# Nine mix products held to the end of the first aggregation, the one-tile group's gate work moved on, and a fetch marker for TensorE's branch

## The chip, the core and the metric

One core of one Trainium2 chip runs the kernel. The metric is device time in microseconds of one execution; the span in the profile runs from the first to the last instruction of the program. TensorE is called PE below, VectorE DVE, ScalarE ACT, GpSimd POOL and SyncE SP.

## What is computed

A graph of 3125 nodes (25 tiles of 128 rows, the last of 53) with 53125 weighted edges, 256 features a node. In short:

```python
xn = layernorm(x)
spmm = lambda z: segment_sum(edge_weight[:, None] * z[src], dst)     # A @ z
h = spmm(xn)                                                         # first aggregation
A0 = softmax(spmm(h) @ W0.T + b0); A1 = softmax(spmm([A0, A0]) @ W1.T + b1)
gnn = tanh(concat([A0, A1]) + h)                                     # 4 equal heads, mean
mix = linear attention of xn, folded to xn @ M + bo                  # M is 256 x 256
x = x + gnn + mix
probs = softmax(layernorm(x) @ gate_w + gate_b)                      # 8 experts
idx = argmax(probs); pos = place of the token in its expert's queue, kept if pos < 489
x = x + expert_ffn(idx, layernorm(x)) * probs[idx] * kept            # 256 -> 1024 -> 256
```

## The kernel before, in words

Five engine programs run side by side and meet at semaphores. Each engine takes its instructions in the order written.

**Build and first aggregation.** `UNITS` are 163 pieces of the dense adjacency matrix (strips of 512 columns of 4 tiles; strip 5 has 3 tiles, strip 6 the tiles 23 and 24). One loop over `it` runs on every engine. For each unit DVE makes one-hot operands (`hots`), PE multiplies them into a PSUM bank (`build`, L1555), ACT copies the block to the ring buffer and stores it to HBM (`evac`), and PE applies it to the normalised features (`apply`, L1571) into the banks `ACC` and `ACC + 1` (3 and 4). After a strip ACT and DVE copy these banks out (`strip_out`), and for each tile PE transposes and projects (`hidden_node`, L1463, L1587, L1588) and DVE copies the result (`hn_out`). Between these stand the mix products: `mix(m)` on PE (L1595) multiplies tile m of the transposed features by M, two f32 matmuls, which the profile shows as four instructions, and `mixed(m)` on DVE (L1113) adds the result to `X1`. `MIX_AT` places `mix(0)` to `mix(21)` at it = 40, 44, ..., 124. After the loop PE's order is mix(22), hidden_node(23), mix(23), hidden_node(24), mix(24).

**The branch.** A general path for unusual edge lists stands behind `more_rounds(pe)` (L458, L459): PE loads the register `rounds`, compares, and jumps over the whole body. With the inputs given the body isn't run. SP, POOL and DVE have the same branch over bodies of their own.

**Second and third aggregation.** `strip(l, k, inserts)` (L1720) runs 25 products per strip against adjacency chunks that SP reads back from HBM into a ring of five slots (L586); l = 0 has 7 strips, l = 1 has 8 (`Z1`). In strips 5, 6 and 7 of l = 1, named ka, kb and kc, the tiles are [20, 21], [22] and [23, 24]. Work for earlier strips is put between the products by `inserts`, keyed by the product's number j. `turns` (L1736) multiplies a finished strip by W1, DVE and ACT make the softmax (`biased` L1282, `ex` L852, `summed` L1291, `tanh` L858, `finished` L1298), `gate_turn` (L1463) transposes, ACT copies (`xtout`, L869), `logits` (L1756) multiplies by the gate weights, DVE picks the expert (`chosen`), `counts` (L1765 and on) makes running counts on PE, `slotted` (L1362 to L1366) makes the row numbers, and POOL scatters the rows (L686, L693). Tiles 22, 23 and 24 form one gate group. `zout` (L845) is ACT's copy of a finished strip. After that PE runs 11 filler products (`WARM`, L1823) and the eight experts (L1808, L1820), which need the scattered rows read back (`tokens`) and transposed (L1448).

Of the kernel before, what the change touches and what calls it, by code (L numbers as in the profile page):

```python
# [16 lines left out]
D = 256  # L17
H = 128
P = 128
NT = 25  # L20
# [103 lines left out]
for _t in range(NT - 2):  # L124
    _k, _i = _t // 4, _t % 4
    HN_AT[NT * _k + 30 + (5 * _i if _k < 5 else _i)] = _t
MIX_AT = {40 + 4 * _m: _m for _m in range(NT - 3)}
KV_AT, T1_AT, M_AT, FOUND_AT = 33, 37, 39, 60

def ge(eng, semaphore, value):

    if not isinstance(value, int) or value > 0:
        eng.wait_ge(semaphore, value)

def graph_program(nc, a, out):
    ctx = ExitStack()
    with ctx:
# [17 lines left out]
        XN, X1 = XX[:, :, 0:D], XX[:, :, D:2 * D]  # L157
        kp, ids = XX[:, :, 2 * D], XX[:, :, 2 * D + 1].bitcast(I32)
        XT = sb("XT", [P, 2, NP])
# [114 lines left out]
        rounds = sb("rounds", [1, 1], I32)  # L274
# [15 lines left out]
        M = W[:, 3364:3876].rearrange("p (c n) -> p c n", c=2)  # L290
# [25 lines left out]
        ps = ctx.enter_context(nc.psum_tensor("ps", [P, 8, 512], F32))  # L316
# [6 lines left out]
        HNB = 5  # L323
        MIXB = 6
        TURN = (2, 7)
        mix_bank = lambda m: MIXB if m < NT - 2 else ACC + m - (NT - 2)
        XTB = 3
        LGB = 5
        CNB = 6
# [125 lines left out]
        @contextmanager  # L455
        def more_rounds(eng):

            count = eng.value_load(rounds[0:1, 0:1], min_val=1, max_val=2)  # L458
            with eng.If(count > 1):  # L459
                with eng.Fori(1, count) as k:  # L460
                    yield k
# [252 lines left out]
        def _(act):  # L714
# [123 lines left out]
            def zout(l, k):  # L838
                w = width((STRIPS, Z1)[l][k])
                act.wait_ge(s_zc, Z_ENDS[l][k])  # L840
                ge(act, s_zt[l], k - 1)
                if l == 0:
                    nc.scalar.activation(zts[k % 2][:, 0:w], ps[:, k % 2, 0:w], ACT.Identity, bias=cols[:, 0:1]).then_inc(s_zev[l], 1)
                else:
                    nc.scalar.copy(zts[k % 2][:, 0:w], ps[:, k % 2, 0:w]).then_inc(s_zev[l], 1)  # L845
# [9 lines left out]
            def tanh(l, k):  # L855
                w = len((STRIPS, Z1)[l][k])
                act.wait_ge(s_sum[l], k + 1)
                nc.scalar.activation(tbuf[k % 2][:, 0:w, :], tbuf[k % 2][:, 0:w, :], ACT.Tanh).then_inc(s_tanh[l], 1)  # L858
# [13 lines left out]
            def exp8(k):  # L872
                t = slice(GATES[k][0], GATES[k][-1] + 1)
                act.wait_ge(s_tb, k + 1)
                nc.scalar.activation(ta8[:, t, :], tb8[:, t, :], ACT.Exp).then_inc(s_exp8, 1)
# [19 lines left out]
            zout(1, kb)  # L895
            ex(1, kb)
            tanh(1, kb)
            exp8(ka)
            xtout(kb)
            zout(1, kc)  # L900
            ex(1, kc)
            tanh(1, kc)
            xtout(kc)
# [21 lines left out]
        def _(dve):  # L925
# [182 lines left out]
                v.tensor_copy(Y[:, t, :], ps[:, HNB, D:D + H]).then_inc(s_hrd, 1)  # L1108

            def mixed(m):  # L1110
                dve.wait_ge(s_mixp, m + 1)
                dve.wait_ge(s_bo, m + 1)
                v.tensor_tensor(X1[:, m, :], X1[:, m, :], ps[:, mix_bank(m), 0:D], ALU.add).then_inc(s_mrd, 1)  # L1113

            heads = lambda x: x.rearrange("p (h d) -> p h d", d=HD)
            g_v = gvb[:, 0, :].unsqueeze(1).to_broadcast([P, 2, HD])
# [94 lines left out]
                if it - 3 in MIX_AT:  # L1211
                    mixed(MIX_AT[it - 3])
            strip_out(NS - 1)
            mixed(NT - 3)
            hn_out(NT - 2)
            mixed(NT - 2)
            hn_out(NT - 1)
            mixed(NT - 1)

            with more_rounds(dve):
# [238 lines left out]
        def _(pe):  # L1460
# [128 lines left out]

            def mix(m):  # L1590
                pe.wait_ge(s_mv, 1)
                if m < NT - 2:
                    ge(pe, s_mrd, m)
                for c in range(2):
                    last = nc.tensor.matmul(ps[:, mix_bank(m), 0:D], XT[:, c, m * P:(m + 1) * P], M[:, c, :], start=(c == 0), stop=(c == 1))  # L1595
                last.then_inc(s_mixp, 1)

            turn(0)
# [1 line left out]
            for it in range(NU + 4):  # L1600
# [40 lines left out]
                    hidden_node(HN_AT[it])  # L1641
                if it in MIX_AT:
                    mix(MIX_AT[it])
            mix(NT - 3)
            hidden_node(NT - 2)
            mix(NT - 2)
            hidden_node(NT - 1)
            mix(NT - 1)

            with more_rounds(pe):
                pe.wait_ge(s_hrd, NT)
                pe.wait_ge(s_mrd, NT)
                pe.sem_inc(m_mm, 1)
                pe.sem_inc(m_app, 1)

                def edges(start):
                    for q in range(8):
                        last = nc.tensor.matmul(ps[:, q, 0:CHUNK], e_dot, e_row[:, q * CHUNK:(q + 1) * CHUNK], start=start, stop=True, skip_group_check=True)
                    last.then_inc(m_mm, 1)  # L1660
                with pe.Fori(0, NT) as j:
                    pe.wait_ge(m_add, j + 1)
                    pe.wait_ge(m_pair, j * ET + 1)
                    edges(True)
                    with pe.Fori(1, ET) as c:
                        pe.wait_ge(m_pair, j * ET + c + 1)
                        edges(False)
                pe.wait_ge(m_add, NT + 1)

                def rows(w, tiles, loaded, across=512, first=0):  # L1670
                    pe.wait_ge(m_chunk, loaded)
                    for i, j in enumerate(tiles):
                        for dd in range(2):
                            last = nc.tensor.matmul(ps[:, ACC + dd, 0:w], XN[:, j, dd * H:(dd + 1) * H], e_chunk[:, i * across + first:i * across + first + w],
                                                    start=(j == 0), stop=True, skip_group_check=True)
                    last.then_inc(m_app, 1)

                def outs(k, w):
                    pe.wait_ge(m_hev, k + 2)
                    for i in range(w):  # L1680
                        pe.wait_ge(m_hrd, k * 4 + i + 1)
                        nodes(hTs[0], i)
                        last_of_nodes[0].then_inc(m_hnt, 1)
                with pe.Fori(0, NS - 1) as k:
                    pe.wait_ge(m_hev, k + 1)
                    for c in range(5):
                        rows(512, range(c * 5, c * 5 + 5), (k * 5 + c + 1) * 16)
                    outs(k, 4)
                pe.wait_ge(m_hev, NS)
                rows(LAST, range(0, ENDN), 31 * 16, ENDW, P)  # L1690
                rows(LAST, range(ENDN, NT), 32 * 16, ENDW, P)
                outs(NS - 1, 1)
                pe.wait_ge(m_hrd, NT + 1)

            def strip(l, k, inserts):
# [30 lines left out]
            def turns(l, k):  # L1727
                b = k % 2
                pe.wait_ge(s_zev[l], k + 1)
                if k >= 2:  # L1730
                    pe.wait_ge(s_ex[0] if l == 0 else s_nm[1], k - 1)
                elif l == 1:
                    pe.wait_ge(s_ex[0], NS - 1 + k % 2)
                for i in range(len((STRIPS, Z1)[l][k])):
                    o, z = ps[:, TURN[b], i * P:(i + 1) * P], zts[b][:, i * P:(i + 1) * P]
                    last = flip(o, z) if l == 0 else nc.tensor.matmul(o, z, W1T[:, :], start=True, stop=True)  # L1736
                last.then_inc(s_zt[l], 1)

            def gate_turn(k):
                pe.wait_ge(s_x1, k + 1)  # L1740
                ge(pe, s_xtb, k)
                for j in Z1[k][DOT_TILES if k < DOTS else 0:]:
                    i = j - GATES[gate_of(k)][0]
                    for c in range(2):
                        last = flip(ps[:, XTB + i // 2, i % 2 * D + c * P:i % 2 * D + (c + 1) * P], X1[:, j, c * P:(c + 1) * P])
                last.then_inc(s_gturn, 1)

            def logits(k):
                g = gate_of(k)
                pe.wait_ge(s_xtb, k + 1)  # L1750
                pe.wait_ge(s_gwc, 2)
                ge(pe, s_lgr, g)
                for j in Z1[k][DOT_TILES if k < DOTS else 0:]:
                    i = j - GATES[g][0]
                    for c in range(2):
                        last = nc.tensor.matmul(ps[:, LGB, i * NE:(i + 1) * NE], xtb[g % 2][:, i, c * P:(c + 1) * P], gate_w[:, c, :], start=(c == 0), stop=(c == 1))  # L1756
                last.then_inc(s_lg, 1)
# [17 lines left out]
            def later(f, *args):  # L1775
                return lambda: f(*args)
# [12 lines left out]
                    inserts[23] = [later(gate_turn, k - 1)]  # L1789
                strip(1, k, inserts)  # L1790
            strip(1, ka, {1: [later(logits, ka - 2)], 3: [later(turns, 1, ka - 1)], 15: [later(counts, ka - 2)], 21: [later(gate_turn, ka - 1)]})
            strip(1, kb, {3: [later(turns, 1, ka)], 4: [later(logits, ka - 1)], 14: [later(counts, ka - 1)], 22: [later(gate_turn, ka)]})
            strip(1, kc, {4: [later(turns, 1, kb)], 5: [later(logits, ka)], 21: [later(counts, ka), later(gate_turn, kb)]})
            turns(1, kc)
            logits(kb)
            gate_turn(kc)
            logits(kc)
# [52 lines left out]
```

## Time and profile before

| | |
|---|---|
| runs of before | 1148.77, 1150.28 and 1151.73 us, median 1150.28 |
| profiled execution | 1142.74 us, span 1141.0 us, mean granted clock 0.978 |
| PE / DVE / ACT / POOL busy | 94% / 65% / 28% / 14% of the span |
| first aggregation ends on PE | at 594.9 us |
| first product of the second aggregation | at 600.5 us |
| last product of the third aggregation | at 890.6 us |
| first expert product | at 913.3 us |

All places are microseconds from the start of the span. A granted clock of 1.00 is 2.4 GHz and 0.50 is 1.2 GHz. A merged timeline row gives start, duration from the first to the last of its instructions, what it is, and in brackets the idle time ahead of it and what ended that.

### The profile page before, as it was taken

To read this page: it belongs to the slowest core of one execution; us is meant where nothing else is said; L and a number is where in the kernel's file an instruction comes from. 1 tells how busy PE (TensorE), PEld (TensorE's weight loads), DVE (VectorE), ACT (ScalarE), POOL (GpSimd) and SP (SyncE) were. 2 spreads that over 40 slices of the span, in tenths; PEclk is the share of its full clock that TensorE was granted. 3 is DMA by queue.
4 is the path that set the end of the run, shared out by engine and by line. 5 is a ranking of instruction groups with operands and counts; after the bars stand their busy time and mean duration, and the time that the engine had idled before them with its cause. 6 is when DMAs were issued, how large, how long until landed. Compare 5 with 4: busy or idle time off the path is not lost.

```text
span 1141.0 us, 15390 instructions
## 1 busy us (share of the span) xinstructions
PE 1071.9 (94%) x5383; PEld 666.5 (58%) x5383; DVE 738.9 (65%) x1860; ACT 314.7 (28%) x1042; POOL 163.2 (14%) x208
## 2 busy tenths in 40 slices
PE   5869989999999999999979999999998799999995
PEld 3446656656666666666774444644458566666664
DVE  8978999998786887869950111217877445544444
ACT  4657867522222222222210111201112112222220
POOL 1113223301000000000000000000344511111111
PEclk9889999999999999999998999999999899999998
DMA  6111110111324333342348988987994665555510
GB/s 173 16 12 47 47 47 18 76 82 76 146 115 153 122 133 136 131 167 105 139 160 314 361 309 301 358 319 281 311 327 171 179 194 125 136 137 133 147 51 8
DMA packets 78877, 178.60 MB, mean 157 GB/s; under 512 B 33567, under 2 KB 62011, under 8 KB 66639
## 3 DMA queue, kind: packets, MB, share of 16 engines
q1 hardware_dynamic: 67550, 126.16, 34.4%
q10 hardware_dynamic: 7120, 43.34, 9.4%
q0 software_dynamic: 4128, 8.08, 2.0%
q8 instruction: 45, 0.74, 0.3%
q14 instruction: 34, 0.27, 0.1%
HBM read 116.23 MB, written 63.77 MB: 158 GB/s over the span
## 4 chain that ended last, share of the span: by engine, by line
PE 77%; DVE 11%; SPq 4%; issue 4%; ACT 2%; DMA 1%; POOLq 0%; POOL 0%; ACTq 0%; DVEq 0%
PE ps L1720 21%; PE ps L1571 20%; PE ps L1820 10%; PE ps L1808 9%; PE ps L1555 7%; SPq L477 2%; PE ps L1595 2%; PE ps L1530 2%; PE ps L1463 1%; PE ps L1516 1%; PE ps L1550 1%; DVE RING L1096 1%; DVE RING L1087 1%; DVE W L1039 1%; SPq L475 1%
## 5 line engine op out<-in xcount | busy, mean ns | idle before, releaser
L1571 PE MATMUL ps<-RING,XX 128*128 128x512 f32 (+2 forms) x700 | 297.1, 550 | 2.0 <-DVE W L1103 2.0
L1720 PE MATMUL ps<-RING,RY 128*128 128x512 f32 (+4 forms) x750 | 272.1, 520 | 5.7 <-issue 5.7
L1720 PEld LDWEIGHTS ps<-RING,RY 128*128 128x128 f32 x750 | 135.7, 194 | 125.7 <-issue 118.3
L790 ACT COPY RING<-ps 128x512 f32<-128x512 f32 (+3 forms) x163 | 91.0, 559 | 291.6 <-PE ps L1555 266.3
L1571 PEld LDWEIGHTS ps<-RING,XX 128*128 128x128 f32 x700 | 118.1, 191 | 69.9 <-issue 62.1
L1096 DVE TENSOR_TENSOR RING<-RING,RY 128x768 bf16<-128x768 bf16 x275 | 142.7, 560 | 4.0
L1555 PEld LDWEIGHTS ps<-RING 128*128 128x128 bf16 x1575 | 100.6, 97 | 50.0 <-issue 43.3
L1087 DVE TENSOR_TENSOR RING<-iota_p,RY 128x512 bf16<-128x512 bf16 x275 | 114.1, 456 | 18.1 <-PE ps L1555 15.7
L1555 PE MATMUL ps<-RING 128*128 128x128 bf16 (+1 forms) x1575 | 112.9, 217 | 0.0
L916 ACT ACTIVATE RY<-ps,b1T 128x489 f32<-128x489 f32 x64 | 42.8, 669 | 172.4 <-PE ps L1808 172.4
L1436 DVE SCALAR_TENSOR_TENSOR W<-ps,RING,W 128x256 f32<-128x256 f32 (+1 forms) x32 | 15.5, 484 | 99.0 <-PE ps L1820 97.8
L1267 DVE TENSOR_REDUCE nmx<-ps 128x4 f32<-128x512 f32 (+2 forms) x7 | 4.4, 635 | 111.7 <-PE ps L1463 111.7
L686 POOL DMA_INDIRECT xbuf_dram<-XX,sidx x25 | 25.1, 1004 | 326.8 <-DVE sidx L1366 321.0
L709 POOL DMA_INDIRECT out<-W,RING x32 | 31.4, 981 | 189.3 <-DVE W L1443 165.0
L672 POOL TENSOR_TENSOR XX<-XX,bo_b 128x256 f32<-128x256 f32 x25 | 21.3, 851 | 244.3 <-PE ps L1555 244.2
L1820 PE MATMUL ps<-XT,RY 128*128 128x256 f32 (+1 forms) x256 | 55.9, 379 | 0.0
L1820 PE MATMUL ps<-RING,RY 128*128 128x256 f32 (+1 forms) x256 | 55.9, 379 | 0.0
L1530 PE MATMUL ps<-wkvT,XT 128*128 128x512 f32 x100 | 50.3, 628 | 4.9 <-ACT XT L752 4.9
L1808 PE MATMUL ps<-RING,XT 128*128 128x489 f32 x128 | 53.2, 574 | 0.5 <-DVE RING L1448 0.5
L1808 PE MATMUL ps<-RING 128*128 128x489 f32 x128 | 53.1, 573 | 0.0
L1820 PEld LDWEIGHTS ps<-RING,RY 128*128 128x128 f32 (+1 forms) x256 | 47.5, 186 | 9.2 <-issue 1.8
L1820 PEld LDWEIGHTS ps<-XT,RY 128*128 128x128 f32 (+1 forms) x256 | 47.5, 185 | 9.2 <-issue 1.8
(265 smaller groups left out, 1313.5 us busy)
## 6 DMA issues: line engine op xcount, KB each, us to landing
RING<-adj_dram SPq DMA_DIRECT2D x60, 1280.0 KB, 6.4
adj_dram<-RING ACTq DMA_DIRECT2D x30, 1280.0 KB, 4.8
rbuf_dram<-W SPq DMA_DIRECT2D x8, 516.0 KB, 5.1
RING<-rbuf_dram SPq DMA_DIRECT2D x8, 516.0 KB, 4.0
xbuf_dram<-W SPq DMA_DIRECT2D x8, 512.0 KB, 3.2
XT<-in_L_ffn_w SPq DMA_DIRECT2D x16, 256.0 KB, 5.2
XT<-in_L_ffn_w SPq DMA_DIRECT2D x4, 1024.0 KB, 8.6
RING<-in_L_ffn_w SPq DMA_DIRECT2D x16, 256.0 KB, 4.5
```

The costliest lines, as they stand in the source:

```text
L686: gp.indirect_dma_start(xbuf_dram[:, :], bass.IndirectOffsetOnAxis(ap=sidx[:, j:j + 1], axis=0), XX[:, j, 0:D], None, bounds_check=NE * XS ...
L709: gp.indirect_dma_start(out[:, :], bass.IndirectOffsetOnAxis(ap=rbs[0:n, e % 2, c, D + 1:RES].bitcast(I32), axis=0), ybs[0:n, e % 2, c, :] ...
L790: nc.scalar.copy(RING[:, n % 2, at:at + w], ps[:, u % 2, 0:w]).then_inc(s_bev, 1)
L916: nc.scalar.activation(hmT[:, f, 0:CAPX], ps[:, 2 + f % 3, 0:CAPX], ACT.Relu, bias=b1T[:, f, e:e + 1]).then_inc(s_hidv, 1)
L1087: last = v.tensor_tensor(h[:, 0:4:3], every.unsqueeze(1).to_broadcast([P, 2, P, fields.shape[-1]]), wide(fields[:, 0:2], 2), ALU.is_equal)
L1096: last = v.tensor_tensor(h[:, 1:4], h[:, 3:4].to_broadcast([P, 3, P, fields.shape[-1]]), wide(fields[:, 2:5], 3), ALU.mult)
L1530: last = nc.tensor.matmul(ps[:, PROD, :], XT[:, c, m * P:(m + 1) * P], wkvT[:, c, :], start=(c == 0), stop=(c == 1))
L1555: last = nc.tensor.matmul(o[:, c:c + w], piece(0, i, P), piece(1 + f, i, w), start=(f == 0), stop=(f == 2 and j != s))
L1571: last = nc.tensor.matmul(ps[:, ACC + dd, 0:w], XN[:, j, dd * H:(dd + 1) * H], at[:, i * w:(i + 1) * w], start=(j == 0), stop=True, skip_g ...
L1720: last = nc.tensor.matmul(o, (Y if l == 0 else S0)[:, j, :], RING[:, slot_of[g % 5], i * across + first:i * across + first + w], start=(j ...
L1808: last = nc.tensor.matmul(ps[:, 2 + f % 3, 0:CAPX], w1s[s][:, c, f * P:(f + 1) * P], xbT[:, s, c, 0:CAPX], start=(c == 0), stop=(c == 1))
L1820: last = nc.tensor.matmul(o, hmT[:, f, c * P:c * P + n], w2s[s][:, f, :], start=(f == 0), stop=(f == 7))
```

## The change

Three edits.

1. `HELD = 16`: only `mix(0)` to `mix(15)` stay in the loop. `mix(16)` to `mix(24)` run after it. They no longer share one bank: `HELD_AT` gives them halves of the banks MIXB, KVACC, PROD, ACC and ACC + 1, so that none waits for DVE to clear another. DVE adds all nine after its last `hn_out`, waiting for both halves of a bank. Since KVACC and PROD are the banks in which `turns` of the second aggregation writes, `turns(0, 0)` and `turns(0, 1)` get a wait for all 25 additions.
2. `more_rounds(pe)` is written out as a wait, the register load, and a compare-and-branch that carries a hint. The hint's place in the instruction stream (`over_general`) is ahead of `hidden_node(24)`.
3. In strips kb and kc PE's inserts are moved: `counts(ka - 1)` and `gate_turn(ka)` from strip kb to strip kc, `turns(1, kb)` and `logits(ka)` later in strip kc, `counts(ka)` and `gate_turn(kb)` behind `turns(1, kc)`. ACT's `zout(1, kc)` goes ahead of `exp8(ka)` and `xtout(kb)`.

```diff
-MIX_AT = {40 + 4 * _m: _m for _m in range(NT - 3)}
+HELD = 16
+MIX_AT = {40 + 4 * _m: _m for _m in range(HELD)}
...
-        mix_bank = lambda m: MIXB if m < NT - 2 else ACC + m - (NT - 2)
+        HELD_AT = ((MIXB, 0), (MIXB, D), (KVACC, 0), (KVACC, D), (PROD, 0), (PROD, D), (ACC, 0), (ACC, D), (ACC + 1, 0))
+
+        def mix_out(m):
+            bank, at = HELD_AT[max(m - HELD, 0)]
+            return ps[:, bank, at:at + D]
+
+        def mixes_to_bank(m):
+            return m + 1 if m < HELD else max(n for n in range(HELD, NT) if HELD_AT[n - HELD][0] == HELD_AT[m - HELD][0]) + 1
... ACT
+            zout(1, kc)
             exp8(ka)
             xtout(kb)
-            zout(1, kc)
... DVE
-                dve.wait_ge(s_mixp, m + 1)
+                dve.wait_ge(s_mixp, mixes_to_bank(m))
...
             strip_out(NS - 1)
-            mixed(NT - 3)
             hn_out(NT - 2)
-            mixed(NT - 2)
             hn_out(NT - 1)
-            mixed(NT - 1)
+            for m in range(HELD, NT):
+                mixed(m)
... PE
-                if m < NT - 2:
-                    ge(pe, s_mrd, m)
+                ge(pe, s_mrd, min(m, HELD))
...
-            mix(NT - 3)
+            mix(HELD)
             hidden_node(NT - 2)
-            mix(NT - 2)
+            mix(HELD + 1)
+            over_general = pe.mark_branch_hint_location()
             hidden_node(NT - 1)
-            mix(NT - 1)
-
-            with more_rounds(pe):
+            for m in range(HELD + 2, NT):
+                mix(m)
+
+            pe.wait_ge(s_rounds, 1)
+            count = pe.value_load(rounds[0:1, 0:1], min_val=1, max_val=2)
+            pe.br_lt(count, 2, "pe_edges_done", "pe_edges_general").branch_hint(over_general)
+            with nc.body("pe_edges_general", ...), pe.Fori(1, count):
...
+            nc.switch_bb("pe_edges_done")
... turns
+                if l == 0 and k < 2:
+                    pe.wait_ge(s_mrd, NT)
...
-            strip(1, kb, {3: [later(turns, 1, ka)], 4: [later(logits, ka - 1)], 14: [later(counts, ka - 1)], 22: [later(gate_turn, ka)]})
-            strip(1, kc, {4: [later(turns, 1, kb)], 5: [later(logits, ka)], 21: [later(counts, ka), later(gate_turn, kb)]})
+            strip(1, kb, {3: [later(turns, 1, ka)], 4: [later(logits, ka - 1)]})
+            strip(1, kc, {4: [later(counts, ka - 1)], 6: [later(gate_turn, ka)], 13: [later(turns, 1, kb), later(logits, ka)]})
             turns(1, kc)
+            counts(ka)
+            gate_turn(kb)
             logits(kb)
             gate_turn(kc)
             logits(kc)
```

## Rows read from the trace of the kernel before

**Rows 1.** The page, part 1: busy time of each engine.
```profile
PE 1071.9 (94%) x5383; PEld 666.5 (58%) x5383; DVE 738.9 (65%) x1860; ACT 314.7 (28%) x1042; POOL 163.2 (14%) x208
```

**Rows 2.** Stretches: length, PE, PEld, DVE, ACT, POOL busy (instructions), clock, DMA share, GB/s.
```profile
450.00:500.00 50.00, 50.00 (x338) 31.30 (x338) 41.59 (x102) 10.54 (x18) 4.35 (x5) 1.00 0.45 165
515.00:540.00 25.00, 25.00 (x177) 17.37 (x177) 24.52 (x58) 5.74 (x12) 1.74 (x2) 1.00 0.26 107
...
595.00:600.50 5.50, 0.00 (x0) 0.00 (x0) 0.34 (x1) 0.00 (x0) 0.00 (x0) 0.80 0.94 388
600.50:605.10 4.60, 4.57 (x6) 2.02 (x7) 0.00 (x0) 0.00 (x0) 0.00 (x0) 0.50 0.69 235
605.10:609.70 4.60, 4.60 (x12) 2.00 (x11) 0.00 (x0) 0.00 (x0) 0.00 (x0) 1.00 0.98 398
...
895.20:900.80 5.60, 3.05 (x14) 2.56 (x15) 4.63 (x26) 2.34 (x6) 0.00 (x0) 0.50 1.07 327
```

**Rows 3.** The chain in the loop and at its end: start, us, what.
```profile
457.93 0.86 PE ps L1595 x4
...
590.82 0.86 PE ps L1595 x4
...
594.88 5.66 issue
```

**Rows 4.** Lines L458 and L459: duration in ns, first start in us.
```profile
L459 SPq COMPARE_BRANCH  x1: 50/50/50, 482.0 to 482.0; - x1
...
L459 PEldq COMPARE_BRANCH  x1: 6295/6295/6295, 594.1 to 594.1; - x1
L459 DVEq COMPARE_BRANCH  x1: 76/76/76, 596.0 to 596.0; - x1
```

**Rows 5.** Instruction packets in the stretch 597.5 to 600.5 us: packets, MB, share.
```profile
q8 instruction: 1, 0.02, 2.0%
```

**Rows 6.** DVE's timeline at the end of the third aggregation (and one addition).
```profile
594.91 0.42 DVE L1113 TENSOR_TENSOR XX<-XX,ps 128x256 f32<-128x256 f32 x1 [0.24 <-PE ps L1595]
...
883.21 0.29 DVE L1282 TENSOR_TENSOR W<-ps,gb_b 128x128 f32<-128x128 f32 x1 [0.78 <-PE ps L1736]
...
889.50 0.17 DVE L1362 TENSOR_TENSOR wkvT<-ps,last_e 128x16 f32<-128x16 f32 x1 [1.98 <-PE ps L1773]
...
891.74 0.42 DVE L1282 TENSOR_TENSOR W<-ps,gb_b 128x256 f32<-128x256 f32 x1 [1.45 <-PE ps L1736]
```

**Rows 7.** PE's timeline over the strips kb and kc and behind them.
```profile
870.47 2.48 PE L1720 MATMUL ps<-RING,RY 128*128 128x128 f32 x20
876.76 0.19 PE L1765 MATMUL ps<-wkvT,upto_b 128*128 128x32 bf16 x1 [3.81 <-DVEq L1343]
...
879.23 1.06 PE L1463 MATMUL ps<-ident,XX 128*128 128x128 f32 x4
...
883.32 0.95 PE L1756 MATMUL ps<-gate_w,XT 128*128 128x8 f32 x8
884.13 5.18 PE L1720 MATMUL ps<-RING,RY 128*128 128x181 f32 x32
...
890.99 0.71 PE L1736 MATMUL ps<-W1T,W 128*128 128x128 f32 x4 [0.40 <-ACT W L845]
...
897.20 1.88 PE L1756 MATMUL ps<-gate_w,XT 128*128 128x8 f32 x8 [0.74 <-ACT XT L869]
...
900.89 11.95 PE L1823 MATMUL ps<-RY,ident 128*128 128x512 f32 x22
913.31 1.06 PE L1808 MATMUL ps<-RING,XT 128*128 128x489 f32 x2 [0.47 <-DVE RING L1448]
```

**Rows 8.** POOL's timeline: the first scatter of the last gate group.
```profile
902.76 0.97 POOL L686 DMA_INDIRECT xbuf_dram<-XX,sidx  x1 [7.99 <-DVE sidx L1366]
```

**Rows 9.** SP's timeline: the loads of strip kc's two chunks.
```profile
868.96 3.23 SPq L586 DMA_DIRECT2D RING<-adj_dram  x2
```

**Rows 10.** Line L586, all chunk loads: time from issue to landing.
```profile
DMA to landing us min/median/max: 5.3/6.3/13.0
```

More of the change, by code:

```diff
@@ L1110, in mixed @@
             def mixed(m):
-                dve.wait_ge(s_mixp, m + 1)
+                dve.wait_ge(s_mixp, mixes_to_bank(m))
                 dve.wait_ge(s_bo, m + 1)
-                v.tensor_tensor(X1[:, m, :], X1[:, m, :], ps[:, mix_bank(m), 0:D], ALU.add).then_inc(s_mrd, 1)
+                v.tensor_tensor(X1[:, m, :], X1[:, m, :], mix_out(m), ALU.add).then_inc(s_mrd, 1)
             heads = lambda x: x.rearrange("p (h d) -> p h d", d=HD)
@@ L1591, in mix @@
                 pe.wait_ge(s_mv, 1)
-                if m < NT - 2:
-                    ge(pe, s_mrd, m)
+                ge(pe, s_mrd, min(m, HELD))
                 for c in range(2):
-                    last = nc.tensor.matmul(ps[:, mix_bank(m), 0:D], XT[:, c, m * P:(m + 1) * P], M[:, c, :], start=(c == 0), stop=(c == 1))
+                    last = nc.tensor.matmul(mix_out(m), XT[:, c, m * P:(m + 1) * P], M[:, c, :], start=(c == 0), stop=(c == 1))
                 last.then_inc(s_mixp, 1)
@@ L1643, in _ @@
                     mix(MIX_AT[it])
-            mix(NT - 3)
+            mix(HELD)
             hidden_node(NT - 2)
-            mix(NT - 2)
+            mix(HELD + 1)
+            over_general = pe.mark_branch_hint_location()
             hidden_node(NT - 1)
-            mix(NT - 1)
-            with more_rounds(pe):
+            for m in range(HELD + 2, NT):
[3 more added lines that the diff above has]
+            pe.br_lt(count, 2, "pe_edges_done", "pe_edges_general").branch_hint(over_general)
+            with nc.body("pe_edges_general", valid_engines=bass.OrderedEngineSet([pe.engine])), pe.Fori(1, count):
                 pe.wait_ge(s_hrd, NT)
```

## The prediction

> **What bounds the kernel now.** I read the page's busy shares first: PE works 94% of the span and no other engine over 65% [rows 1], so what counts is where PE stands still or runs at a low clock, and which engine it then waits for. Next come the stretches. From 450 to 500 us, where the last mix products of the loop stand, PE is busy 50.00 of 50 us while DVE has 8 us free; from 515 to 540 us PE is still full, but DVE is nearly so too [rows 2]. The reader is to see that the loop is paced by PE in both. Then the chain: a mix product is worth 0.86 us of PE in the loop and 0.86 us behind it, and behind the last one stands the longest idle piece of the PE-bound part, 5.66 us put down to "issue", which is no semaphore [rows 3]. The rows of the branch's line name it: the compare-and-branch takes 0.05 us on SP, 0.08 on DVE and 6.30 us on PE, from 594.1 us on [rows 4]. In that time one packet of instructions comes in, late, while the DMA engines are 94% busy at 388 GB/s with chunk loads and stores [rows 2, 5]. Behind the hole the granted clock is 0.50 (1.2 GHz) until 605.1 us, and PE does six instructions in 4.6 us where it then does twelve [rows 2]. Last come the timelines of the end of the third aggregation. From 870 us on PE is no longer the bound: it waits 3.81 us for DVE's one-hot rows with strips kb and kc still to do, and then DVE waits for PE three times, 0.78, 1.98 and 1.45 us, before its last softmax starts at 891.74 us [rows 6, 7]. The chain from there to the first expert product at 913.31 us goes through DVE, ACT, PE, POOL's scatter and the read-back, and each link waits for the one before.
>
> **Edit 1, the held products.** Six products (16 to 21) leave the loop: 6 x 0.86 = 5.16 us of PE come off a stretch in which PE never waits [rows 2, 3]. The same six come back behind the loop, again 5.16 us, with PE full on both sides. Sum 0. DVE loses six additions of 0.42 us [rows 6] from the loop, where they were hidden; one of them, for product 21, falls into the stretch where DVE is nearly full, so at most 0.42 us is gained there; I take 0. At the end DVE makes nine additions, 9 x 0.42 = 3.8 us and about 0.5 us for the last one after PE's last product. Queued behind them on DVE is only its branch and the first reduction of the second aggregation, which needs `turns(0, 0)`. The new wait for all 25 additions stands in `turns(0, 0)`, behind 25 + 8 products of strip 0 and 1: at twelve instructions in 4.6 us [rows 2] and two instructions a product that is 66 x 0.38 = 25 us after the first product. It costs nothing; if the cover were gone it would cost the half microsecond. The products write six different half banks and wait for no addition after the sixteenth, so PE runs them at 0.86 us each. SP's queue: its chunk loads are released by the last build and the last apply, both 5.16 us earlier, and PE's first strip starts about as long after them as now, so that the loads have the same lead.
>
> The Trainium skill (Runtime: NRT & Kernel Launch, Instruction fetch mechanics) says that a taken branch whose target is not in the fetch window forces a DMA fetch before execution can go on. The trace agrees: 6.30 us and a packet of instructions. The same section says "Prefetch is purely sequential"; by that rule the marker could not bring the target early, and edit 2 would be worth 0; no row here has a marked branch.
>
> **Edit 3, the gate work.** In the trace's own time, from 870.47 us on. PE does the last 20 products of strip kb in one go: twice the 2.48 us of ten of them gives 875.4 us, where now the wait of 3.81 us stands between. Strip kc's 25 products are 50 instructions at 5.18/32 = 0.162 us, 8.1 us. Between them go counts(ka - 1), whose one-hots come at 876.76 us, when PE is at kc's fifth product (877.0), so it doesn't wait; gate_turn(ka), at most 1.06 us; turns(1, kb), 0.4; logits(ka), 0.95 [rows 7]. Strip kc ends at about 886.1 us instead of 890.6. These durations hold the tails of pipelined groups; by the instructions' distance it is 884.7.
>
> DVE decides the rest. Its order is unchanged. It is free for kb's softmax 0.78 us before it gets turns(1, kb), and turns(1, kb) is now done by about 881 us, so 0.78 us is saved. slotted(ka) then waits for counts(ka), which PE now has behind turns(1, kc): ACT's copy at 885.0 to 886.4, turns(1, kc) 0.7 us [rows 7], counts at 885.9 to 887.5. DVE asks for it at 889.50 - 1.98 - 0.78 = 886.74 us [rows 6]. So of the 1.98 us between 1.2 and all is saved. turns(1, kc) is then long done, and the 1.45 us are saved too. The sum is 3.4 to 4.2 us [rows 6]; I take 4.0, nearer the end that the instructions' distance gives. ACT's moved copy is what lets turns(1, kc) run before xtout(kb); xtout(kb) and exp8(ka) have until the last logits. POOL's queue: the scatter of the last group starts 7.99 us after POOL's last work [rows 8] and may come 4 us earlier without a collision. SP's queue: the loads of kc's two chunks are released by kb's fifth and tenth product, which do not move. The first is needed at 875.4 us; a load takes 5.3 to 13.0 us, median 6.3, from 868.96 us on [rows 9, 10], so the median lands in time and the slowest would be 6.6 us late. The filler products take 11.95 us and end 0.5 us before the experts can start [rows 7]; they move with the chain. But behind 895.2 us the clock is at 0.50 [rows 2], and if it rises later against the chain than now, the fillers end up to 1 us late; if it is at 1.00 the last logits, 1.88 us for eight against 0.95 for eight [rows 7], win 0.9 us. I take 0 and keep 1 us either way for the range.
>
> **The sum.** 0 + 5.66 + 2.3 + 4.0 = 12.0 us. The profiled execution would go from 1142.74 to 1130.7 us. The runs of before have a median 7.5 us above that execution; I take the difference as the same and get 1150.28 - 12.0 = 1138.3 us.
>
> **The rivals.**
> - The marker does nothing: PE stands 5.7 us at the branch and the clock falls as now. For it: nothing in the trace shows a fetch asked for ahead. Against it: between marker and branch there are 6.9 us and the fetch needs 6.3. Time: 1150.28 - 4.0 = 1146.3 us. A fetch that lands late by some microseconds gives a time between this and the forecast, and is counted here. Chance 0.13. The Trainium skill's rule of sequential prefetch, named above, would lead to this case.
> - The gate work gives nothing, because PE waits for kc's first chunk (a landing near the maximum of [rows 10]), or the counts come late. Time: 1150.28 - 7.9 = 1142.4 us. Against it: landings are mostly near the median. Chance 0.09.
> - Slower: the marked fetch takes the place of the block that PE needs next in sequence. PE then runs dry among the held products, for 6.30 us [rows 4] with the clock falling behind it (2.3 us), and the branch still costs its 5.7 and 2.3 us. It decides only if both fetches are paid: 1150.28 - 4.0 + 8.6 = 1154.9 us. Against it: PE's ordinary block fetches leave no hole in 50 us of loop [rows 2]. Chance 0.05.
> - Both gains fail and nothing is lost: about 1150 us, chance 0.05.
>
> **How the numbers follow.** The forecast has 0.68; its own range is 1136 to 1141 us (gate work 3.4 to 4.2, 0.4 us in the loop, 1 us of clock either way, 1 us of measurement). With the two cases of one gain the range is 1135.5 to 1146.5 us, which leaves out 0.15. A change under 0.3% (3.5 us) can't be told from none in this kernel. Faster by more: 0.68 + 0.13 + 0.09 = 0.90, less a case of a weak single gain, 0.89. Within 0.3%: 0.06. Slower: 0.05.
>
> **What the profile after would show.** The branch's row on PE at some 0.1 us in place of 6.3, no idle piece behind the last mix product, and a clock of 1.00 through the first strip. The last apply about 5.2 us earlier and nine mix products in a row with hidden nodes between, 0.86 us each. No wait for L1765 in strip kb; DVE's idle time ahead of L1282 and L1362 gone, and 21.6 us from the start of the last softmax (L1282) to the first expert product, as now. It is wrong if the branch's row stays at microseconds, if a hole opens elsewhere in the held products, if L1720 waits for a chunk in strip kc, or if the filler products end after the transposes.

## The result, and the profile after

The changed kernel takes 1138.07 us (median of 4 runs, 1137.69 to 1140.0) beside 1150.36 us of before: 12.3 us less between the medians. The ratio of the means is 0.9897 (interval 0.988 to 0.9914), which is 11.8 us. The forecast was 1138.3 us and 12.0 us less. All ratios below leave out three executions of early_marker that took 1864 to 4980 us, and the profile of the first of them, at a granted clock of 0.56, is not used.

The profile of this run, though, is only 4.6 us shorter than the profile shown of before: the span is 1136.4 us against 1141.0. So it has to be read by stages. Four places cut the span: the first mix product (first L1595, now L1601), the first product of the second aggregation and the first of the third (L1720, now L1732), and the first expert product (L1808, now L1824).

| stage, us | before | after | difference |
|---|---|---|---|
| start to first mix product | 266.22 | 265.02 | -1.2 |
| to the second aggregation | 334.31 | 328.61 | -5.7 |
| second aggregation | 136.92 | 134.66 | -2.3 |
| third aggregation and gate, to the first expert | 175.86 | 180.42 | +4.6 |
| experts to the end | 227.69 | 227.69 | 0.0 |

The first stage holds no changed work, so its 1.2 us are not the change's. The next two are the hole (PE's idle time at its branch) and the clock behind it, to the tenth of a microsecond. The fourth is longer where 4 us less were forecast. First the part that went as said. These are the stretches of the loop and behind it, with columns as in [rows 2]:

```profile
450.00:500.00 50.00, 50.00 (x337) 29.77 (x336) 42.91 (x105) 11.15 (x19) 5.07 (x5) 1.00 0.47 175
515.00:540.00 25.00, 25.00 (x178) 17.05 (x177) 24.56 (x60) 6.11 (x13) 0.92 (x1) 1.00 0.38 158
585.00:593.60 8.60, 8.60 (x46) 7.19 (x45) 4.23 (x12) 0.00 (x0) 0.00 (x0) 1.00 1.00 384
593.60:598.60 5.00, 5.00 (x13) 2.37 (x13) 0.45 (x2) 0.00 (x0) 0.00 (x0) 1.00 0.59 199
```

PE is full in the loop as before [rows 2], full through the held products, and the second aggregation starts at a clock of 1.00. PE's timeline shows the seam, and the rows of the two lines show marker and branch (duration in ns, first start in us):

```profile
587.49 6.21 PE L1601 MATMUL ps<-W,XT 128*128 128x256 f32 x28
593.63 2.81 PE L1732 MATMUL ps<-RING,RY 128*128 128x512 f32 x6
```

```profile
L1653 PEldq BRANCH_PREFETCH_HINT  x1: 55/55/55, 585.1 to 585.1; - x1
...
L1661 PEldq COMPARE_BRANCH  x1: 2918/2918/2918, 590.5 to 590.5; - x1
```

Seven products in 6.21 us, and no idle time ahead of L1732, where [rows 3] had 5.66 us. But the branch takes 2.92 us and not 0.1. It starts at 590.5 us, when PE still has 3.2 us of products in its queue, and so hides: the sequencer, which takes in PE's instructions and runs the branch (its rows are those of PEldq), is that far ahead of the array. Now the part that did not go as said, DVE's timeline and PE's over the strips kb and kc:

```profile
868.29 0.42 DVE L1305 TENSOR_TENSOR XX<-XX,W 128x256 f32<-128x256 f32 x1
...
874.05 0.19 DVE L1369 TENSOR_TENSOR wkvT<-ps,last_e 128x32 f32<-128x32 f32 x1 [1.83 <-remote]
...
886.40 0.17 DVE L1369 TENSOR_TENSOR wkvT<-ps,last_e 128x16 f32<-128x16 f32 x1 [6.35 <-remote]
```

```profile
862.07 6.25 PE L1732 MATMUL ps<-RING,RY 128*128 128x128 f32 x50
...
868.43 0.18 PE L1787 MATMUL ps<-wkvT,ones_b 128*128 128x32 bf16 x1
...
872.39 0.47 PE L1732 MATMUL ps<-RING,RY 128*128 128x181 f32 x2 [0.96 <-issue]
...
883.74 0.17 PE L1787 MATMUL ps<-wkvT,ones_b 128*128 128x16 bf16 x1
```

The 3.81 us wait for the counts is gone, PE runs 50 instructions in 6.25 us. But L1369 waits for L1787, the last product of `counts`, and starts at 874.05 us where that product is on record at 868.43, and at 886.40 where it is at 883.74. The profile calls the releaser "remote": it finds no event that fits. These late signals are in neither the prediction nor the profile of before. The question for the experiments was whether the 12 us are those that were argued, and what the late signals do to them.

### The profile page after: what moved, and what is told of

It is laid out like the page before. It is cut to its first block, busy times and chain, and to the rows that moved or that the text cites. A ratio compares the mean times of both kernels' runs of the same rounds, so it can differ in the third digit from the quotient of the medians.

```text
span 1136.4 us, 15395 instructions
## 1 busy us (share of the span) xinstructions
PE 1071.8 (94%) x5383; PEld 666.0 (59%) x5383; DVE 739.0 (65%) x1860; ACT 315.2 (28%) x1042; POOL 160.9 (14%) x208
## 4 chain that ended last, share of the span: by engine, by line
PE 77%; DVE 12%; SPq 4%; issue 3%; ACT 2%; another core or an unknown queue 1%; DMA 1%; POOLq 0%; DVEq 0%
PE ps L1578 20%; PE ps L1732 20%; PE ps L1836 10%; PE ps L1824 9%; PE ps L1562 7%; PE ps L1601 2%; SPq L485 2%; PE ps L1537 2%; PE ps L1523 1%; PE ps L1470 1%; PE ps L1557 1%; DVE RING L1104 1%; PE ps L1839 1%; DVE RING L1095 1%; DVE W L1047 1%
## 5 line engine op out<-in xcount | busy, mean ns | idle before, releaser
L1732 PE MATMUL ps<-RING,RY 128*128 128x512 f32 (+4 forms) x750 | 271.1, 518 | 1.8 <-issue 1.6
L1732 PEld LDWEIGHTS ps<-RING,RY 128*128 128x128 f32 x750 | 135.3, 193 | 121.2 <-issue 113.7
L1824 PE MATMUL ps<-RING,XT 128*128 128x489 f32 x128 | 53.2, 574 | 0.4 <-issue 0.4
L1824 PE MATMUL ps<-RING 128*128 128x489 f32 x128 | 53.1, 573 | 0.0
```

Source lines behind the costliest of these rows:

```text
L1732: last = nc.tensor.matmul(o, (Y if l == 0 else S0)[:, j, :], RING[:, slot_of[g % 5], i * across + first:i * across + first + w], start=(j ...
L1824: last = nc.tensor.matmul(ps[:, 2 + f % 3, 0:CAPX], w1s[s][:, c, f * P:(f + 1) * P], xbT[:, s, c, 0:CAPX], start=(c == 0), stop=(c == 1))
```

## The experiments

Ratios are to before on the same chip, in the same hours. Before took 1151.13 us on one chip and 1143.25, 1142.55 and 1143.46 us on three others. All stages below are from one profile each.

### Before again

> The kernel before, unchanged, for a second profile and for the noise. The profiled execution of before took 1142.74 us and its timed runs 1148.8 to 1151.7 us; the profile of the changed kernel took 1138.14, a typical time of it. Theory A (both parts of the change gain in each execution): a new profile of before of 1149 to 1151 us has its extra 7 to 8 us ahead of strip kb of the third aggregation, spread over the stages. Theory B (late signals): in the profile of the changed kernel PE's semaphore increments came 3 to 6 us late in two places behind strip kb, which cost about 8 us; a typical execution of before has such places too, and its extra 7 to 8 us lie between strip kb and the first expert product, whose distance is 46 us in the fast profile. Ratio of the times 1.000 in both.

Ratio 0.9986 (0.9974 to 0.9998), profile of 1148.2 us. The stages are 266.08, 334.42, 136.89, 183.17 and 227.69 us: all of the extra 7 us lie in the fourth. The waits of DVE from 860 to 905 us, first here, then in the first profile of before (total us, times, longest):

```profile
DVE W L1282 <- remote: 7.7, 2, 7.2
...
DVE wkvT L1331 <- remote: 2.6, 1, 2.6
DVE W L1282 <- PE ps L1736: 0.8, 1, 0.8
```

```profile
DVE wkvT L1362 <- PE ps L1773: 2.5, 2, 2.0
DVE W L1282 <- PE ps L1736: 2.2, 2, 1.5
```

So the late signals belong to before as much as to after. Five profiles have them: this one, that of the changed kernel and those of the next three experiments. The first profile of before and the eight later ones have none. The two levels of before, 1151 and 1143 us, fit this: the profile with late signals is of an execution of 1150.65 us, the one without of 1142.74 us. That it holds for the three chips at 1143 us is argued from other kernels' profiles there, since before wasn't profiled on them. The baseline for the changed kernel's first profile is this one, not the one shown ahead: against it the stages differ by -1.1, -5.8, -2.2, -2.8 and 0 us, together 11.9. Of these 10.8 us lie in stages with changed work.

### Held products and marker, gate work as it was

```diff
 (the changed kernel)
-            zout(1, kc)
             exp8(ka)
             xtout(kb)
+            zout(1, kc)
... and the inserts of strips kb and kc as before
```

> Held products and marker (edits 1 and 2), with the gate work where it was. Theory A: 7.9 us faster than before (5.66 of the hole behind the branch, 2.3 of the clock), about 1142.4 us, branch row under 3 us and no idle piece ahead of the first product of the second aggregation. Theory B agrees on this part; it differs on what edit 3 then adds. Rival C (layout: the whole gain comes from where PE's work falls against the late signals): not 7.9 but anything from 0 to 12 us.

Ratio 0.9927 (0.9913 to 0.994), 8.4 us. The stages are 266.97, 328.79, 134.66, 183.81 and 227.60 us: -5.6 and -2.2 us in the second and third against before again, 7.9 us with the hole gone and the clock kept. The branch's row is 3.04 us where under 3 was expected, and of the hole 0.15 us is left (595.61 to 595.76):

```profile
591.78 3.83 PE L1601 MATMUL ps<-W,XT 128*128 128x256 f32 x17
595.76 4.53 PE L1732 MATMUL ps<-RING,RY 128*128 128x512 f32 x10
```

### The gate work alone

```diff
 (the kernel before)
-            strip(1, kb, {3: [later(turns, 1, ka)], 4: [later(logits, ka - 1)], 14: [later(counts, ka - 1)], 22: [later(gate_turn, ka)]})
...
+            strip(1, kb, {3: [later(turns, 1, ka)], 4: [later(logits, ka - 1)]})
...
```

> The gate work moved (edit 3) alone. Theory A: 3.4 to 4.2 us faster than before, about 1146.3 us; the distance from the last instruction of strip kb's first five products to the first expert product falls from some 43 to some 39 us. Theory B: the gain in an execution depends on whether PE's signals come late behind strip kb: where they do in both kernels, 4 us are still gained; where they come late only in the changed order, because PE no longer rests in strip kb, up to 4 us are lost against the fast profile of before.

Ratio 0.9969 (0.9958 to 0.9981), 3.6 us; the fourth stage is 178.66 us against 183.17, so 4.5 us less. The two parts add up: 8.4 + 3.6 = 12.0, measured together 11.8. This profile has late signals too (DVE waits for L1362 2.0 and 3.6 us), so the 4.5 us are a difference between two stages with late signals; after_again, below, gives the size without them.

### The marker alone, 1.7 us of work ahead of the branch

```diff
 (the kernel before)
             mix(NT - 2)
+            over_general = pe.mark_branch_hint_location()
             hidden_node(NT - 1)
             mix(NT - 1)
... the branch as in the changed kernel
```

> The marker alone, put ahead of hidden_node(24), with only that and mix(24) between it and the branch, 1.7 us of PE work. Theory A (the marker starts the fetch): the branch's row falls from 6.3 us by 1.7 to 2.5 us, to some 4 us, the hole from 5.66 to some 3.5 us; the clock may still fall; 2 to 4 us faster. Rival (the marker does nothing, and the sequencer was only further ahead in the changed kernel): the row stays at 6.3 us and the time at that of before.

Ratio 0.9991 (0.9982 to 1.0001): nothing that can be told. The branch's row:

```profile
L1654 PEldq COMPARE_BRANCH  x1: 5558/5558/5558, 592.0 to 592.0; - x1
```

The marker stands at 589.16 us, so the target was there 8.4 us behind the marker, where an unmarked branch has it after 6.3 (6.40 in before again). The marker's 2.9 us ahead bought 0.8 us of branch; the hole is 5.06 us. The expectation of 1.7 to 2.5 us was wrong: the fetch is not of a fixed length. Most of the 0.7 us of hole is lost again behind it: the granted clock is 0.50 from 596.5 to 603.4 us, and as PE's products start at 597.75 us, more of them fall under it than in before. The second aggregation takes 137.46 us, 0.6 more than in before again.

### The held products alone

```diff
 (the changed kernel, gate work as before)
-            over_general = pe.mark_branch_hint_location()
...
-            pe.br_lt(count, 2, "pe_edges_done", "pe_edges_general").branch_hint(over_general)
...
+            with more_rounds(pe):
```

> The nine held products (edit 1) alone, with the branch as before. Theory A: no change, since PE is full where the six products leave and where they come back: ratio 1.000 within the 0.15% by which before repeats itself; the branch's row stays near 6.3 us, the hole near 5.7 us or, as PE's sequencer now runs up to 3 us ahead of the products without a wait, some 3 us. In the second case 2 to 3 us of the gain put down to the marker belong to the held products. Rival: held products cost their 5.2 us, ratio 1.0045.

Ratio 0.995 (0.9935 to 0.9964), 5.7 us faster: the expected ratio of 1.000 failed, and the second case of the hole came. PE's timeline and the branch's row:

```profile
588.90 6.21 PE L1601 MATMUL ps<-W,XT 128*128 128x256 f32 x28
597.91 6.66 PE L1727 MATMUL ps<-RING,RY 128*128 128x512 f32 x11 [2.80 <-issue]
```

```profile
L467 PEldq COMPARE_BRANCH  x1: 5742/5742/5742, 591.9 to 591.9; - x1
```

PE's products end at 595.11 us against 594.88 in before, so they themselves cost nothing. But seven products without a wait let the sequencer run ahead. It reaches the branch 3.2 us before PE runs dry, where [rows 3, 4] had 0.8, and the hole is 2.80 us. The low clock behind it is shorter too: the granted clock is back at 1.00 by 602.2 us, and the second aggregation takes 136.36 us, 0.6 less. Hole and clock make 2.9 + 0.6 = 3.5 us. The timed 5.7 us (4.1 to 7.4) are more than that; what the rest is, this profile doesn't show.

### The marker alone, early

```diff
 (the kernel before, branch as in the changed kernel)
             for it in range(NU + 4):
+                if it == NU:
+                    over_general = pe.mark_branch_hint_location()
                 if it < NT:
```

> The kernel before with the marked branch alone, the marker four iterations ahead of the loop's end, some 9 to 10 us of PE work ahead of the branch; no product is held. Theory A (all that counts is that the fetch starts more than 6.3 us ahead): the branch's row under 3 us, no or little hole (PE's sequencer is only 0.8 us ahead there, so up to 2 us may be left), 5 to 8 us faster, about 1143 us. Rival (the held products are what closes the hole): no more than the marker alone gave, 1150 us.

Ratio 0.9926 (0.9907 to 0.9945). The rows are those of the same kernel's second profile:

> Before with the marker alone, four iterations ahead of the loop's end, for a profile at full clock (the first one of this kernel was taken in a disturbed execution at a clock of 0.56). Branch row 0.1 to 0.5 us, since in four profiles the target was there 7.7 to 9.7 us behind the marker and here some 9.7 us of work stand between; hole under 0.5 us, clock 1.00 through the first strip, ratio 0.993.

Ratio 0.9926 (0.9908 to 0.9944), 8.5 us. PE's timeline and the branch:

```profile
593.91 1.03 PE L1595 MATMUL ps<-W,XT 128*128 128x256 f32 x4
594.96 5.39 PE L1726 MATMUL ps<-RING,RY 128*128 128x512 f32 x12
```

```profile
L1655 PEldq COMPARE_BRANCH  x1: 493/493/493, 594.3 to 594.3; - x1
```

No hole, the second and third stage are 328.66 and 134.67 us, and no product was moved. The whole gain of edits 1 and 2 is to be had from the marker. What the held products did in the change was to put the marker 5.5 us ahead of the branch on the sequencer where marker_only has 2.9, and to lengthen PE's queue at the branch from 0.8 to 3.2 us.

### The scatters left out, and some moved

The first of these two kernels leaves the scatters of gate groups 0 to 5 out, so that the experts get mostly blank rows; the second moves four of them.

```diff
 (the changed kernel, POOL; in the first, waits for s_disp and s_dres count the last group alone)
-            for k in range(NGT - 2):
-                scatter(k)
-                scatter_rest(k)
...
+            scatter(NGT - 1)
+            scatter_rest(NGT - 1)
```

> The changed kernel without the scatters of the first six gate groups; only the last group's rows are scattered, the waits count those alone, so the experts work on mostly blank rows. Theory D (PE's signals come late behind strip kb while GpSimd's scatters are under way, and only then): no PE signal over 1 us late, the stretch from strip kb to the first expert product falls from 49.9 to some 43 us, 5 to 8 us faster than the changed kernel, about 1131 us. Rival E (they come late from PE's own dense short instructions or from the chunk loads): late signals stay, 1137 to 1138 us.

```diff
 (the changed kernel, POOL)
-            for k in range(NGT - 2):
+            for k in range(NGT - 3):
                 scatter(k)
                 scatter_rest(k)
... and NGT - 3 in the two loops behind it
```

> The changed kernel with the second scatters (the residual rows) of gate group 4 moved behind the last group's first scatters. Theory D: four scatters fewer while strips kb and kc run, so fewer late signals, 1 to 4 us faster than the changed kernel, about 1135 us; the residual rows of expert 0 come 5 us later, still ahead of their use some 14 us after the first expert product. Rival E: the same as the changed kernel, or slower by the wait of DVE for the residual rows.

Ratios 0.9861 (0.9843 to 0.9879) and 0.9886 (0.9866 to 0.9906), on a chip where held_only has no late signal either. Both fail as tests of the cause: there was nothing to take away. Against the changed kernel run again (below) the first is shorter by 3.5 us in its span, and the experts to the end alone, with 224.09 us against 227.62, make these 3.5; of the other stages the first is 0.6 us shorter and the fourth 0.7 longer. That the blank rows cause it is likely, and wasn't looked into. Its fourth stage is 172.06 us, not shorter than 171.33. So where no signal is late, the scatters beside the strips cost nothing that the stages show. In the second kernel's profile the branch takes 2.14 us and leaves no hole, with the marker where the change has it.

### The changed kernel again

> The changed kernel, unchanged, beside the two below. So far before took 1151 us on one chip, whose profiles have late PE signals behind strip kb, and 1143 us on another, whose profiles have none. Theory A: on either, 12 us faster than before, ratio 0.9890; where no signal is late, the stretch from strip kb to the first expert product is 41.5 to 42.5 us against 46.1 in the first profile of before, where it is disturbed some 50 against 52.5. Theory B (the late signals give the gain): ratio 0.993 on a chip without them.

Ratio 0.9901 (0.9885 to 0.9917), 1132.06 against 1142.55 us. The stages are 266.77, 329.99, 134.66, 171.33 and 227.62 us. This is the profile to hold against the one of before: no signal is late in either. PE's timeline, then DVE's:

```profile
589.22 6.21 PE L1601 MATMUL ps<-W,XT 128*128 128x256 f32 x28
596.76 3.67 PE L1732 MATMUL ps<-RING,RY 128*128 128x512 f32 x8 [1.33 <-issue]
...
864.45 6.25 PE L1732 MATMUL ps<-RING,RY 128*128 128x128 f32 x50
870.74 0.19 PE L1779 MATMUL ps<-wkvT,upto_b 128*128 128x32 bf16 x1
...
879.74 0.17 PE L1779 MATMUL ps<-wkvT,upto_b 128*128 128x16 bf16 x1
...
890.49 12.43 PE L1839 MATMUL ps<-RY,ident 128*128 128x512 f32 x22
902.75 1.80 PE L1824 MATMUL ps<-RING,XT 128*128 128x489 f32 x4
```

```profile
876.30 0.29 DVE L1289 TENSOR_TENSOR W<-ps,gb_b 128x128 f32<-128x128 f32 x1
...
880.64 0.17 DVE L1369 TENSOR_TENSOR wkvT<-ps,last_e 128x16 f32<-128x16 f32 x1
...
881.35 0.41 DVE L1289 TENSOR_TENSOR W<-ps,gb_b 128x256 f32<-128x256 f32 x1
```

The three rows of DVE are those of [rows 6], and none has a bracket any more: the 0.78, 1.98 and 1.45 us are all gone. In the seam the branch takes 4.34 us here, and 1.33 us of hole are left, at a clock of 1.00.

> Four second scatters moved behind the last first scatters, as in rest_later, now beside the changed kernel. If the scatters make PE's signals late: 1 to 4 us faster than after_again on a chip with late signals, equal on one without. If they have no part in it: equal on both, ratio within 0.15% of after_again's.

Ratio 0.9896 (0.9879 to 0.9913), fourth stage 171.54 us against 171.33: the same as after_again, on a chip without late signals. What makes them is not told apart.

### The changed kernel with its marker early

```diff
 (the changed kernel)
-            over_general = pe.mark_branch_hint_location()
...
             for it in range(NU + 4):
+                if it == NU:
+                    over_general = pe.mark_branch_hint_location()
```

> The changed kernel with its marker at the fourth iteration from the loop's end, some 14 us of PE work ahead of the branch, instead of ahead of hidden_node(24). The target was there 7.7 to 9.8 us behind the marker in six profiles, against 6.3 us behind an unmarked branch; with the marker where the change has it, 0 to 1.35 us of hole were left. So: branch row under 0.5 us, hole under 0.1 us, up to 1.3 us faster than the changed kernel, ratio to before 0.989 on a chip without late signals (after_again had 0.9901 there). Rival (the block fetched early is gone again by the time of the branch, since PE takes in a further block of its own on the way): the row back at 6 us and a hole of 2.8 us as with held products alone, ratio 0.992.

Ratio 0.988 (0.9861 to 0.9898), 1129.67 us beside 1143.46. The branch's row is 0.40 us, and the hole is gone:

```profile
586.84 6.21 PE L1601 MATMUL ps<-W,XT 128*128 128x256 f32 x28
592.88 7.46 PE L1733 MATMUL ps<-RING,RY 128*128 128x512 f32 x17
```

Its second stage is 328.49 us against 329.99 of after_again, 1.5 us less. Part of it is lost again: the second aggregation takes 135.21 us against 134.66, and PE waits in it for a chunk that SP reads back, once, at 641 us, which no other profile has:

```profile
PE ps L1733 <- DMA RING<-adj_dram: 0.4, 1, 0.4
```

The intervals of the two ratios overlap, so the gain of the hole is shown by the rows, and that the whole is faster is not shown by the times. The rival, a target that is gone again by the time of the branch, didn't come. But it was hardly tested: from 580.5 to 593 us the trace has no instruction packet, so PE took in no other block between the target's and the branch.

## Why the prediction was right, point by point

**Edit 1, the sum of 0.** Right for the products (nine of them in nine half banks, where I wrote six): in held_only they end 0.23 us later than in before, with a first stage 0.23 us later too. Wrong for the edit as a whole, which alone gave 5.7 us. The step that failed is "PE's sequencer reaches the branch 0.8 us before the last product's end": I took this lead from before's order and kept it for the changed one, where it is 3.2 us. The 25 additions' wait cost nothing: the second aggregation has no idle time on PE ahead of its `turns` and takes 134.66 us.

**Edit 2, the hole.** "If the fetch is started at the marker it has landed when PE gets there, and the branch costs what it costs DVE, 0.08 us" was wrong twice. The marker-to-branch distance is 5.4 to 5.6 us on the sequencer in six profiles, not 6.9. The products from marker to branch do take 6.9 us of PE (in after_again from 588.53 to 595.43), but the sequencer is 1.7 us ahead of them at the marker and 3.2 us at the branch. And the target came 7.7 to 9.8 us behind the marker, not 6.3. So 2.1 to 4.3 us of branch were left. The hidden lead of 3.2 us swallowed all of it in the first profile and all but 1.33 us in the second. The sum's 5.66 us came out at 5.7 and 4.3 because two errors stood against each other; with the lead of 0.8 us that I had written, 1.3 to 3.5 us would have been left. So far the hit is luck. The credit is wrong too: the held products take 2.9 us of the hole without any marker.

**The clock.** Right: 2.3 us of [rows 2], measured 2.26 us (136.92 to 134.66) in both profiles of the changed kernel. Of the six other profiles with a hole of 1.35 us or less five have 134.58 to 134.67 us, and after_marker_early 135.21. The lower bound, a clock that falls anyway, did not come.

**Edit 3.** Right in its mechanism, and 0.5 us under-sized (after_again against the first profile of before). The last softmax starts 20.17 us behind strip kb's first product (861.18) against 24.53 us in before (867.21), 4.4 us where 3.4 to 4.2 were given; the first expert product comes 4.5 us earlier. kb and kc took what the instructions' distance said, not the durations: kb's last 20 products and kc ended at 878.8 us, 17.6 us behind kb's start against 23.4. All of the 1.98 us went, not 1.2. The filler products now end the stage: in before they ended 0.5 us ahead of the first expert product, here L1824 follows them at once. The prediction named this as a sign of being wrong. It cost little: the first expert product starts 0.99 us behind the first transpose (901.76 to 902.75 us), where in before it was 0.86 us (912.45 to 913.31).

**The sum and the baseline.** I made the sum against a profile of 1141.0 us and took the 7.5 us to the median as the same in both kernels. For the profile that failed: it was to take 1130.7 us and took 1138.14, 0.07 us from its median. Between medians the difference did hold: the ratio is 0.9897 where signals are late and 0.9901 where they are not. I had no reason for it from the trace, and the shape of the gain differs: 5.8 or 4.3 us of hole, 2.2 or 2.3 us of clock, 2.8 or 4.5 us of gate work. These make 10.8 or 11.1 us, not 12.0.

**The rivals.** No rival's time came about. But half of the first did: it counted "a fetch that lands late by some microseconds", and that is what happened in all six profiles with the change's marker, hidden, wholly in three of them and for the most part in the others, by a lead that neither the forecast nor the rival had. The marker does work: early_marker_2 has 0.49 us against 6.30. This is also the answer to the Trainium skill's sentence that prefetch is purely sequential (Runtime: NRT & Kernel Launch, Instruction fetch mechanics): a marked target comes in ahead of the branch, so the sentence does not hold for a branch with a hint. Its other sentence, that a far target forces a fetch, holds in all four profiles with an unmarked branch on PE (5.74 to 6.40 us). No chunk came late for strip kc, and no second fetch made a hole among the held products; between marker and branch the instruction queue moved only one packet, so this rival wasn't put to a test.

## What to carry to other kernels

- A far branch on a busy engine has three terms: when its fetch starts, how long the fetch takes in the DMA traffic of that moment, and how much work is queued in the engine when the sequencer gets there. Read the last from the branch's start against the end of the last product, in the order that will stand there, not in the one that does. Put the marker ahead of the large transfers, since behind them its packet came up to 4 us later: the plainest version, one marker and nothing moved, gave all 8 us.
- When the profiled execution stands several microseconds off the median, find the stage that holds the difference before a sum is made against it. A second profile of the same kernel costs little.
- Work that an in-order queue holds behind a wait is worth moving even when that queue isn't the bound: the idle brackets on the engine that is bound give the price, here 4.2 us read and 4.4 measured.

## What the runs showed of the hardware

**The fetch of a far target depends on what was handed to the DMA engines before it.** With the marker at 583.0 us (early_marker_2) the engines were 5% busy until 586.3 us, when the second of two instruction packets moved; with the marker at 586.8 us (after_again) they were 100% busy, and a single packet moved only behind 594 us. The stretches, columns as in [rows 2]:

```profile
583.00:586.30 3.30, 3.30 (x40) 3.25 (x37) 1.58 (x6) 0.92 (x2) 0.00 (x0) 1.00 0.05 10
```

```profile
586.80:594.20 7.40, 7.40 (x42) 6.38 (x41) 3.50 (x10) 0.00 (x0) 0.00 (x0) 1.00 1.00 377
```

And the instruction queue of after_again from 594 to 597 us, where there is none from 586 to 594:

```profile
q8 instruction: 1, 0.02, 2.0%
```

But busy engines alone don't make the wait: an unmarked branch finds them as busy and waits less. What goes with the wait is how long before the request the last of three large transfers was issued (two chunk loads of 1280 KB each and a store of 995 KB):

| asked for by | engines busy meanwhile | last large issue before it | packet moves after |
|---|---|---|---|
| marker, early_marker_2 and after_marker_early | 2% and 0% | 4.4 us, a store alone | 3.3 and 3.5 us |
| branch, held_only | 91% | 7.5 us | 3.4 us |
| branch, before | all the time | 4.7 us | 4.0 us |
| marker, marker_only | all the time | 2.0 us | 6.1 us |
| marker, the six profiles with it where the change has it | all the time | 2.1 us | 5.4 to 7.4 us |

From the start of the packet to the end of the branch it is 2.33 to 2.37 us in all eleven profiles in which the branch stood waiting, so all of the spread lies ahead of the packet. That the packet waits behind the transfers issued before it is the reading that fits; the queue itself isn't on record, and why the last row spreads over 2 us with the same 2.1 us is open.

**PE's signals came 2 to 7 us late in some profiles.** Five profiles have this, all behind 845 us, while small products, chunk loads and scatters run together. On the one chip known for it, four kernels of four had it; on the three others none of eight. Which chip the first two profiles come from isn't on record: before's has no late signal, the changed kernel's has. The fourth stage of before is 7.3 us longer with them. Those profiles also miss some 600 to 700 of about 8800 records of semaphores, most of them of DMA, with some of DVE, ACT and PE, so that the recording itself may have a part in it. The experiments with the scatters ran on chips without it and leave its cause open.
